# Layer 1 of a graph network: edge products are laid into the gather's destination and the gather adds to them

## Chip, core and metric

One core of one Trainium2 chip. The metric is device time in microseconds (us) of one execution, median of several runs. Engines are named as in the profile: PE (TensorE), DVE (VectorE), ACT (ScalarE), POOL (GpSimd, which also issues the gathers), SP (SyncE, which issues the plain transfers).

## What is computed

Four layers on a graph of 3125 nodes with 256 features and 50,000 edges sorted by target. The change is in layer 1, a graph transformer with 8 heads of 32:

```
h   = relu(layernorm(x))
q, k, v, skip = h@Wq.T+bq, h@Wk.T+bk, h@Wv.T+bv, h@Wskip.T+bskip
e   = edge_attr @ We.T                       # per edge, 64 -> 256
k_e = k[src] + e ;  v_e = v[src] + e
a   = sum_c(q[dst] * k_e) / sqrt(32)          # per head
w   = softmax of a over the edges of one dst
x  += segment_sum(v_e * w, dst) + skip
```

## The kernel before

`dense_phase(layer=1)` computes q, k, v and skip in 25 tiles of 125 nodes. Queries stay in SBUF. A table in HBM (`table_kv`) gets, for each node, the 256 keys and then, in 8 heads of 33 columns, value minus key and a column of ones (`moved`): 520 words a row.

`blend_phase` then walks the edges. The edge list is padded to 448 steps of 125 edges; G = 4 steps are a block, B = 4 blocks a chunk, so there are 28 chunks and 112 blocks. Per block:

- POOL gathers four times 128 rows of the table into `rows` (L1335), two chunks ahead at most: it waits until the block that used the buffer two chunks before is summed (`summed`).
- PE, `ask`: `queries` times a one-hot matrix gives q[dst] in PSUM (L1436); ACT copies it to `asked` (L1397).
- PE, `keys`: attributes times We (L1449) and, on top of it in the same PSUM bank `ps_k`, identity times the gathered keys (L1452): k[src] + e. In fp32 each product is two recorded MATMULs.
- DVE, `offer`: keys times queries (L1530), and (v - k) + (k + e) (L1532), which is the value with its edge part. `judge` sums the first per head (L1538).
- PE, `part`: a small product for layer 3 (L1462), moved out by DVE `lift`.
- Once per chunk a running maximum per target is carried over the steps: transposes on PE, scans on DVE (L1594 to L1626), ended by L1603, which signals `peaked`.
- DVE, `message`: values and ones times the weight (L1552); PE, `total`: one-hot times messages (L1471, signals `summed`); DVE, `add`: into the accumulator (L1564).

These are pipelined by hand. Each engine's `body(c, h)` runs the four slots b = 0 to 3 of chunk c in one loop; in slot b PE asks and keys the block LEAD = 6 blocks ahead and totals block b. SP loads, per chunk, the one-hot places (488 KB), lanes and flags, then for each block two pieces of attributes of 62.5 KB (L1224, semaphore `attrset[b]`). Its order for chunk c:

```
if not known(c, 2):
    keep(c - 2, h)
    sp.wait_ge(broad, (c - 1) * B)
    sp.wait_ge(peaked, c - 1)
...
sp.dma_start(places[:, h], targets[...]).then_inc(loaded[h], 16)
load_borders(sp, borders, lane, flag, c, h, laned)
...
    load_attributes(nc, sp, c, b, word, [...], attr_t, attrset[b])
```

`peaked` reaches c - 1 in DVE's slot b = 3 of the loop three chunks before c.

## Time and profile before

| | |
|---|---|
| median of 3 runs | 3252.54 us (3248.59 to 3256.95) |
| profiled execution, its own time | 3248.09 us |
| its span, first to last instruction | 3246.0 us |
| mean granted TensorE clock | 0.865 |
| busy over the span: PE, DVE, ACT, POOL | 78%, 71%, 52%, 47% |
| blend stage of layer 1 | about 760 to 1736 us |

The busy shares are means over stages with different limits, so the blend stage is read by itself. A row's "idle before" is the time in which the engine had nothing to do just ahead of that group, and the arrow names what ended the wait; "issue" is time with no visible cause.

### The profile page before, as it was taken

The numbers are of one execution on the slowest core, as the hardware profiler recorded it, in microseconds if no ns is written. First come the engines' busy times: TensorE is split into PE (matmuls) and PEld (weight loads), VectorE is DVE, ScalarE is ACT, GpSimd is POOL, SyncE is SP. The second block draws the span as 40 slices with busy tenths as digits, with TensorE's granted clock in tenths as the row PEclk, the third lists the DMA queues.
The fourth block names the chain that finished last, engine by engine and source line by source line (L and its number), as shares of the span: only waits on it lengthen the run. The fifth ranks groups of instructions, "written<-read, shape, count | busy, mean of one in ns | idle before, by whom it ended". The sixth has DMA issues, their size and how long they took to land. (4 is left out here: it accounts for less than half of the span.)

```text
span 3246.0 us, 56122 instructions
## 1 busy us (share of the span) xinstructions
PE 2527.9 (78%) x12612; PEld 1928.6 (59%) x12613; DVE 2300.0 (71%) x5860; ACT 1696.6 (52%) x4048; POOL 1516.6 (47%) x1759
## 2 busy tenths in 40 slices
PE   2999998596999999999984488887860577878870
PEld 1888887444666666666663366666650455666650
DVE  4788887574788788778775367676778466766767
ACT  1666665322555555555552466666641466666651
POOL 1333333103444555455440377777730377777740
PEclk9999999798999999999996678778875777878885
DMA  2100000225556666565640355555522455555521
GB/s 68 24 10 8 10 9 9 60 67 177 152 159 166 161 164 165 153 168 159 164 122 24 113 134 139 137 139 137 139 60 35 116 142 142 142 142 141 142 64 39
DMA packets 186874, 349.20 MB, mean 108 GB/s; under 512 B 74641, under 2 KB 117034, under 8 KB 186507
## 3 DMA queue, kind: packets, MB, share of 16 engines
q0 software_dynamic: 83520, 249.39, 30.4%
q1 hardware_dynamic: 103239, 98.62, 10.5%
q14 instruction: 84, 0.68, 0.1%
q8 instruction: 31, 0.51, 0.1%
HBM read 325.45 MB, written 22.44 MB: 107 GB/s over the span
## 5 line engine op out<-in xcount | busy, mean ns | idle before, releaser
L1759 POOL DMA_INDIRECT t_rows<-table_h,t_istage x896 | 854.6, 954 | 266.0 <-issue 248.6
L1846 PE MATMUL t_pso<-t_rows,t_hot 125*125 125x272 f32 (+1 forms) x1792 | 597.3, 489 | 104.6 <-DVE t_rows L1885 64.3
L1335 POOL DMA_INDIRECT b_rows<-table_kv,b_istage x448 | 458.8, 1024 | 378.5 <-PE b_pso L1471 252.9
L1846 PEld LDWEIGHTS t_pso<-t_rows,t_hot 125*125 125x125 f32 x1792 | 402.7, 236 | 202.5 <-issue 105.5
L1397 ACT COPY b_asked<-b_psq 125x512 f32<-125x512 f32 x224 | 131.1, 585 | 427.6 <-PE b_psq L1436 427.6
L1885 DVE TENSOR_TENSOR t_rows<-t_rows,t_psm 125x1056 f32<-125x1056 f32 x224 | 276.7, 1235 | 63.5 <-issue 63.4
L1832 PE MATMUL t_pss<-node_scores,t_hot_t 125*125 x1792 | 266.2, 279 | 33.7 <-ACT t_hot_t L1790 31.1
L1832 PEld LDWEIGHTS t_pss<-node_scores,t_hot_t 125*125 125x125 f32 x1792 | 260.5, 225 | 49.1 <-issue 44.1
L1797 ACT ACTIVATE t_hot<-con_iota,g_dstl 125x125 f32<-125x125 f32 x896 | 280.3, 384 | 0.0
L1895 DVE TENSOR_TENSOR acc<-acc,t_pso 125x272 f32 (+1 forms) x448 | 192.7, 430 | 118.2 <-DVE acc L1895 69.1
L1436 PE MATMUL b_psq<-queries,b_hot_t 125*125 x896 | 235.6, 386 | 45.4 <-issue 23.7
L1452 PE MATMUL b_psk<-b_rows,con_ident 125*125 125x256 f32 x896 | 256.4, 409 | 0.0
L1471 PE MATMUL b_pso<-b_rows,b_hot 125*125 125x264 f32 x896 | 236.0, 408 | 17.4 <-DVE b_rows L1552 17.4
L1530 DVE TENSOR_TENSOR b_rows<-b_psk,b_asked 125x1024 f32<-125x1024 f32 x112 | 136.5, 1218 | 151.2 <-PE b_psk L1452 151.2
L1788 ACT ACTIVATE t_hot_t<-t_places,t_minus 125x500 f32<-125x500 bf16 x224 | 156.5, 699 | 108.5 <-PE t_pss L1832 77.8
L1436 PEld LDWEIGHTS b_psq<-queries,b_hot_t 125*125 125x125 f32 x896 | 163.1, 190 | 76.1 <-issue 51.6
L1452 PEld LDWEIGHTS b_psk<-b_rows,con_ident 125*125 125x125 f32 x896 | 151.7, 189 | 89.2 <-issue 76.2
L1148 PE MATMUL d_pso<-wt,d_ht 128*125 128x512 f32 (+1 forms) x400 | 160.1, 545 | 44.6 <-DVE d_stage L1010 19.1
L1471 PEld LDWEIGHTS b_pso<-b_rows,b_hot 125*125 125x125 f32 x896 | 164.8, 194 | 46.3 <-issue 19.7
L1449 PE MATMUL b_psk<-we,b_attr 64*125 64x256 f32 x896 | 158.8, 430 | 22.2 <-issue 12.6
L1790 ACT ACTIVATE t_hot_t<-t_hot_t,con_ones 125x500 f32<-125x500 f32 x224 | 159.4, 712 | 7.3
L1801 ACT ACTIVATE t_hot<-t_hot,con_ones 125x500 f32<-125x500 f32 x224 | 159.4, 712 | 7.3
(394 smaller groups left out, 4961.5 us busy)
## 6 DMA issues: line engine op xcount, KB each, us to landing
t_places<-targets SPq DMA_DIRECT2D x56, 488.3 KB
t_rows<-table_h,t_istage POOLq DMA_INDIRECT x896, 3.7
b_attr<-in_attr_t SPq DMA_DIRECT2D x224, 62.5 KB
b_places<-targets SPq DMA_DIRECT2D x28, 488.3 KB
b_rows<-table_kv,b_istage POOLq DMA_INDIRECT x448, 5.4
table_h<-d_stage SPq DMA_DIRECT2D x50, 132.8 KB
t_flag<-flags SPq DMA_DIRECT2D x56, 62.5 KB
table_kv<-d_moved SPq DMA_DIRECT2D x25, 128.9 KB
```

The lines of the kernel that those rows point to most:

```text
L1148: mm = pe.matmul(ps_o[u % 3][0:P, lo:hi], ht[:, u, a, :], weight[:, a, lo:hi], start=(a == 0), stop=(a == 1))
L1335: pool.indirect_dma_start(out=rows[:, h, s, :], out_offset=None, in_=table, in_offset=bass.IndirectOffsetOnAxis(ap=istage[:, h, s:s + 1], ...
L1436: mm = pe.matmul(ps_q[0:P, w * D:(w + 1) * D], hot_t[:, b % 2, v * PAIR + w, :], q, start=True, stop=True)
L1452: mm = pe.matmul(to(u), ident[0:P, 0:P], rows[0:P, h, b * G + u, 0:D], start=False, stop=True)
L1471: mm = pe.matmul(ps_o[0:P, at:at + MW], hot[:, h, b * G + u, :], rows[0:P, h, b * G + u, D:WIDE], start=u % PAIR == 0, stop=u % PAIR == PA ...
L1759: pool.indirect_dma_start(out=rows[:, r, s, :], out_offset=None, in_=table, in_offset=bass.IndirectOffsetOnAxis(ap=istage[:, r, s:s + 1], ...
L1790: act.activation(x, x, ACT.Relu, scale=-1.0, bias=con["ones"][0:P, 0:1]).then_inc(hot_ts, 1)
L1797: act.activation(hot[:, r, b * G + u, :], con["iota"][0:P, 0:P], ACT.Abs, scale=-1.0, bias=g["dstl"][:, bass.ds(n * G + u, 1)]).then_inc(d ...
L1832: mm = pe.matmul(expanded[:, b * G + u], hot_t[:, b % 2, u, :], ntab[:, bass.ds(ts[u // PAIR], 1), 0:nw].rearrange("p a d -> p (a d)"), st ...
L1846: mm = pe.matmul(ps_o[b % 2][0:P, at:at + mw], hot[:, r, b * G + u, :], rows[0:P, r, b * G + u, 0:mw], start=u % PAIR == 0, stop=u % PAIR ...
L1885: dve.tensor_tensor(v, v, weight[:, b * G:(b + 1) * G].unsqueeze(3).to_broadcast([P, G, H, HW]), ALU.mult).then_inc(mset, 1)
L1895: dve.tensor_tensor(row, row, ps_o[b % 2][0:P, v * 512:v * 512 + mw], ALU.add).then_inc(added, 1)
```

## The change

1. The table's row is keys and values side by side, 512 words, without ones; `moved`, its subtraction and one of the two stores of each tile go.
2. PE forms only the edge product (`edges`), two blocks earlier than `keys` did: REACH = 8 blocks ahead of the slot, where `ask` stays at 6. The identity products go.
3. The product is copied from PSUM twice into the block's rows, once for the keys and once for the values, 7 blocks ahead (`spread`): ACT's `lay` copies two halves for blocks 1 and 2, one for blocks 0 and 3, whose other half DVE copies (`lend`). Each copy reads 512 words a partition and writes 1024.
4. The gather takes 125 rows of 512 words and adds them to what lies there (`compute_op=ALU.add`); it waits for `laid` and, in blocks 0 and 3, `lent`.
5. `offer` is one multiplication, SBUF by SBUF, and waits for the gather; the addition goes. ACT writes the exponential weights straight into the rows' last 8 columns; messages have 32 columns a head, and the denominator is its own 8 columns.

```diff
...
                         dve.wait_ge(evac, n + 1)
-                        parts = lambda k: stage[:, u, k * D:(k + 1) * D].rearrange("p (h c) -> p h c", h=H)
-                        dve.tensor_tensor(moved[:, u, :].rearrange("p (h c) -> p h c", h=H)[:, :, 0:C], parts(2), parts(1), ALU.subtract).then_inc(lined, 1)
...
                             if layer == 1:
-                                sp.wait_ge(lined, n + 1)
-                                sp.dma_start(tables[0][bass.ds(n * P, P), 0:D], stage[:, u, D:2 * D]).then_inc(stored[u], 16)
-                                sp.dma_start(tables[0][bass.ds(n * P, P), D:D + MW], moved[:, u, :]).then_inc(stored[u], 16)
+                                sp.wait_ge(evac, n + 1)
+                                sp.dma_start(tables[0][bass.ds(n * P, P), :], stage[:, u, D:3 * D]).then_inc(stored[u], 16)
...
     WIDE = D + MW
+    REACH = 2 * B
+    SHARED = (0, B - 1)
...
         istage = sb("istage", [ROWS, 2, RUN], I32)
-        rows = sb("rows", [ROWS, 2, RUN, WIDE])
+        rows = sb("rows", [P, 2, RUN, WIDE])
...
         asked = sb("asked", [P, 2, G, D])
...
+        def lent_by(c, b):
+            return 2 * c + (2 if b else 1)
+        def spread(to, bank, h, b, v):
+            s = b * G + v * PAIR
+            edge = bank[0:P, v * 512:(v + 1) * 512].rearrange("p (u d) -> p u d", u=PAIR)
+            return to(rows[:, h, s:s + PAIR, 0:2 * D].rearrange("p u (k d) -> p u k d", k=2), edge.unsqueeze(2).to_broadcast([P, PAIR, 2, D]))
...
                     for b in range(B):
-                        if not known(c, 2):
-                            pool_wait(pool, summed, (c - 2) * B + b + 1)
+                        if b in SHARED:
+                            pool.wait_ge(lent, lent_by(c, b))
+                        pool_wait(pool, laid, c * B + b + 1)
...
                             s = b * G + u
-                            pool.indirect_dma_start(out=rows[:, h, s, :], out_offset=None, in_=table,
-                                                    in_offset=bass.IndirectOffsetOnAxis(ap=istage[:, h, s:s + 1], axis=0)).then_inc(gathered[h * B + b], 16)
+                            pool.indirect_dma_start(out=rows[:, h, s, 0:2 * D], out_offset=None, in_=table,
+                                                    in_offset=bass.IndirectOffsetOnAxis(ap=istage[0:P, h, s:s + 1], axis=0), compute_op=ALU.add).then_inc(gathered[h * B + b], 16)
...
+                def lay(c, h, b):
+                    n = c * B + b
+                    act.wait_ge(edged, n + 1)
+                    if not known(c, 2):
+                        act.wait_ge(summed, n - 2 * B + 1)
+                    if b not in SHARED:
+                        spread(act.copy, ps_k[b % 2], h, b, 1)
+                    spread(act.copy, ps_k[b % 2], h, b, 0).then_inc(laid, 1)
...
                     if v == 0 and (b >= 2 or not known(c, 1)):
-                        act.wait_ge(used, n - 1)
+                        act.wait_ge(multiplied, n - 1)
...
                     for b in range(B):
-                        here, ahead, hence = (block_at(c, h, b + k) for k in (LEAD, LEAD + 1, 1))
+                        here, ahead, hence, empty = (block_at(c, h, b + k) for k in (LEAD, LEAD + 1, 1, REACH - 1))
+                        if b == 0 and not known(c, 0):
+                            act.wait_ge(gapped, c + 1)
+                            act.activation(rows[:, h, :, 2 * D:WIDE], gap[:], ACT.Exp, scale=SCALE).then_inc(weighed, 1)
+                        if empty:
+                            lay(*empty)
...
                             ask(*here, 0)
-                        if b == 0 and not known(c, 0):
-                            act.wait_ge(gapped, c + 1)
-                            act.activation(weight[:], gap[:], ACT.Exp, scale=SCALE).then_inc(weighed, 1)
...
                 turn(0, 0, 0)
+                for b in range(B - 1):
+                    lay(0, 0, b)
...
-                def keys(c, h, b, w):
+                def edges(c, h, b, w):
...
-                        pe.wait_ge(gathered[h * B + b], (c - h) * 8 * G + 16 * G)
                         if b >= 2 or not known(c, 1):
-                            pe.wait_ge(used, n - 1)
+                            pe.wait_ge(laid, n - 1)
+                            if b == 2:
+                                pe.wait_ge(lent, lent_by(c, 0))
+                            elif b == 1:
+                                pe.wait_ge(lent, lent_by(c - 1, B - 1))
...
                         half = slice(v * ED, (v + 1) * ED)
-                        pe.matmul(to(v * PAIR + w), attr[half, b, w * P:(w + 1) * P], we[half], start=True, stop=False)
-                    for v in range(GP):
-                        u = v * PAIR + w
-                        mm = pe.matmul(to(u), ident[0:P, 0:P], rows[0:P, h, b * G + u, 0:D], start=False, stop=True)
+                        mm = pe.matmul(to(v * PAIR + w), attr[half, b, w * P:(w + 1) * P], we[half], start=True, stop=True)
                     if w == PAIR - 1:
-                        mm.then_inc(keyed, 1)
+                        mm.then_inc(edged, 1)
...
                     for b in range(B):
-                        here = block_at(c, h, b + LEAD)
+                        here, empty = (block_at(c, h, b + k) for k in (LEAD, REACH))
...
                             ask(*here, 0, word)
-                            keys(*here, 0)
+                        if empty:
+                            edges(*empty, 0)
...
                             ask(*here, 1, word)
-                            keys(*here, 1)
+                        if empty:
+                            edges(*empty, 1)
...
                 word = load_stairs(pe, g, 0)
+                for b in range(B - 1):
+                    for w in range(PAIR):
+                        edges(0, 0, b, w)
                 for b in range(LEAD - B):
-                    ask(0, 0, b, 0, word)
-                    keys(0, 0, b, 0)
-                    ask(0, 0, b, 1, word)
-                    keys(0, 0, b, 1)
+                    for v in range(GP):
+                        ask(0, 0, b, v, word)
                     part(0, 0, b)
+                for w in range(PAIR):
+                    edges(0, 0, B - 1, w)
...
                     n = c * B + b
-                    dve.wait_ge(keyed, n + 1)
+                    dve.wait_ge(gathered[h * B + b], (c - h) * 8 * G + 16 * G)
                     dve.wait_ge(copied, (n + 1) * GP)
-                    mine = rows[0:P, h, b * G:(b + 1) * G]
-                    k = ps_k[b % 2][0:P, :]
-                    dve.tensor_tensor(mine[:, :, 0:D], k.rearrange("p (u d) -> p u d", u=G), asked[:, b % 2], ALU.mult).then_inc(multiplied, 1)
-                    v = mine[:, :, D:].rearrange("p u (h c) -> p u h c", h=H)[:, :, :, 0:C]
-                    dve.tensor_tensor(v, v, k.rearrange("p (u h c) -> p u h c", u=G, h=H), ALU.add).then_inc(used, 1)
+                    k = rows[:, h, b * G:(b + 1) * G, 0:D]
+                    dve.tensor_tensor(k, k, asked[:, b % 2], ALU.mult).then_inc(multiplied, 1)
+                def lend(c, h, b):
+                    dve.wait_ge(edged, c * B + b + 1)
+                    spread(dve.tensor_copy, ps_k[b % 2], h, b, 1).then_inc(lent, 1)
...
                 def message(c, h, b):
-                    n = c * B + b
-                    dve.wait_ge(used, n + 1)
-                    v = rows[0:P, h, b * G:(b + 1) * G, D:].rearrange("p u (h c) -> p u h c", h=H)
-                    dve.tensor_tensor(v, v, weight[:, b * G:(b + 1) * G].unsqueeze(3).to_broadcast([P, G, H, HW]), ALU.mult).then_inc(mset, 1)
+                    mine = rows[:, h, b * G:(b + 1) * G]
+                    v = mine[:, :, D:2 * D].rearrange("p u (h c) -> p u h c", h=H)
+                    dve.tensor_tensor(v, v, mine[:, :, 2 * D:WIDE].unsqueeze(3).to_broadcast([P, G, H, C]), ALU.mult).then_inc(mset, 1)
...
                         if b == 0:
-                            dve.wait_ge(rescaled, c + 1)
+                            dve.wait_ge(rescaled, 2 * c + 2)
...
                                 first = nc.s_assert_within(now & 31, 0, NT - 1, skip_runtime_bounds_check_because="a count of NT - 1 borders")
-                                old = acc[:, bass.ds(first, 1), 0:MW].rearrange("p a (h c) -> p (a h) c", h=H)
+                                old = acc[:, bass.ds(first, 1), 0:D].rearrange("p a (h c) -> p (a h) c", h=H)
+                                share = acc[:, bass.ds(first, 1), D:MW].rearrange("p a h -> p (a h)")
...
                                     dve.wait_ge(added, c * B * GP)
-                                dve.scalar_tensor_tensor(old, factor.unsqueeze(2).to_broadcast([P, H, HW]), 1.0, old, ALU.add, ALU.mult).then_inc(rescaled, 1)
+                                dve.scalar_tensor_tensor(old, factor.unsqueeze(2).to_broadcast([P, H, C]), 1.0, old, ALU.add, ALU.mult).then_inc(rescaled, 1)
+                                dve.scalar_tensor_tensor(share, factor, 1.0, share, ALU.add, ALU.mult).then_inc(rescaled, 1)
...
                             message(c, h, b)
+                        if empty and empty[2] in SHARED:
+                            lend(*empty)
...
                     dve.tensor_copy(split[v * ED:(v + 1) * ED, v], we3[v * ED:(v + 1) * ED]).then_inc(setup, 1)
+                lend(0, 0, 0)
...
             we1, asks = fsb("we1", [128, D]), fsb("queries", [P, NT, D])
-            t1 = dram("table_kv", N, D + MW)
+            t1 = dram("table_kv", N, 2 * D)
...
```

The accumulator's denominator moves with it: the two readers in `dense_phase` take columns D to MW. SP's code in `blend_phase` is as before.

## Rows read from the trace of the kernel before

**Rows 1.** Windows, the blend stage alone: us, busy us of each engine (instructions), PEclk, DMA share.
```profile
812.00:1692.00 880.00, 836.21 (x4075) 599.04 (x4074) 703.03 (x1183) 470.58 (x1009) 433.25 (x441) 0.99 0.59 160
```

**Rows 2.** Groups by line and shape, 740 to 1750 us.
```profile
L1335 POOL DMA_INDIRECT b_rows<-table_kv,b_istage x448 | 458.8, 1024 | 378.5 <-PE b_pso L1471 252.9 <-issue 124.5 <-POOL b_istage L1320 1.2
...
L1452 PE MATMUL b_psk<-b_rows,con_ident 125*125 125x256 f32 x896 | 256.4, 409 | 0.0
...
L1552 DVE TENSOR_TENSOR b_rows<-b_rows,b_weight 125x1056 f32<-125x1056 f32 x112 | 140.1, 1251 | 1.3 <-ACT b_weight L1407 1.3
...
L1530 DVE TENSOR_TENSOR b_rows<-b_psk,b_asked 125x1024 f32<-125x1024 f32 x112 | 136.5, 1218 | 151.2 <-PE b_psk L1452 151.2
...
L1532 DVE TENSOR_TENSOR b_rows<-b_rows,b_psk 125x1024 f32<-125x1024 f32 x112 | 135.6, 1211 | 0.0
...
L1397 ACT COPY b_asked<-b_psq 125x512 f32<-125x512 f32 x224 | 131.1, 585 | 427.6 <-PE b_psq L1436 427.6
```

**Rows 3.** Waits of the engines, 740 to 1750 us: total us, times, longest.
```profile
DVE b_rows L1530 <- PE b_psk L1452: 151.2, 85, 16.1
```

**Rows 4.** Line L1603, all its instructions.
```profile
L1603 DVE TENSOR_TENSOR_SCAN b_most<-b_flag,b_init,b_run x28: 477/478/479, 808.4 to 1705.1; 128x125 f32<-128x125 bf16 x28
```

**Rows 5.** Waits of SyncE's queue, 760 to 1750 us.
```profile
SPq L1352 <- DVE b_most L1603: 335.8, 26, 16.4
```

**Rows 6.** Timeline of one chunk: start us, us, engine, line.
```profile
1199.87 2.02 PE L1471 MATMUL b_pso<-b_rows,b_hot 125*125 125x264 f32 x8
...
1202.67 0.94 POOL L1335 DMA_INDIRECT b_rows<-table_kv,b_istage  x1 [2.39 <-PE b_pso L1471]
...
1203.21 0.40 DVE L1614 COPY b_on<-b_lane_ends 1x8 f32<-1x8 f32 x1
...
1205.50 0.16 DVE L1626 TENSOR_SCALAR b_fade<-b_fade 1x8 f32<-1x8 f32 x1
...
1206.88 1.25 DVE L1552 TENSOR_TENSOR b_rows<-b_rows,b_weight 125x1056 f32<-125x1056 f32 x1
...
1208.94 0.48 DVE L1603 TENSOR_TENSOR_SCAN b_most<-b_flag,b_init,b_run 128x125 f32<-128x125 bf16 x1
...
1209.63 0.29 SPq L1353 DMA_DIRECT2D b_places<-targets  x1
...
1212.72 3.40 SPq L1224 DMA_DIRECT2D b_attr<-in_attr_t  x4
...
1213.80 1.13 PE L1452 MATMUL b_psk<-b_rows,con_ident 125*125 125x256 f32 x4
...
1214.77 1.03 PE L1436 MATMUL b_psq<-queries,b_hot_t 125*125 x4
...
1214.96 1.25 DVE L1552 TENSOR_TENSOR b_rows<-b_rows,b_weight 125x1056 f32<-125x1056 f32 x1
...
1215.22 1.80 POOL L1335 DMA_INDIRECT b_rows<-table_kv,b_istage  x1 [0.30 <-issue]
```

**Rows 7.** DMA queues, 1215.3 to 1218.6 us: packets, MB, share.
```profile
q1 hardware_dynamic: 329, 0.24, 28.4%
```

**Rows 8.** DMA issues of the page: times, median us to landing.
```profile
t_rows<-table_h,t_istage POOLq DMA_INDIRECT x896, 3.7
...
b_rows<-table_kv,b_istage POOLq DMA_INDIRECT x448, 5.4
```

**Rows 9.** DMA queues, 812 to 1692 us.
```profile
q0 software_dynamic: 33280, 110.78, 46.7%
q1 hardware_dynamic: 27189, 29.45, 12.6%
```

**Rows 10.** Window of 3 us in layer 2.
```profile
2015.00:2018.00 3.00, 3.00 (x12) 2.20 (x10) 2.49 (x6) 2.39 (x6) 2.30 (x3) 0.61 0.54 167
```

**Rows 11.** TensorE timeline, layer 2.
```profile
2014.29 3.58 PE L1846 MATMUL t_pso<-t_rows,t_hot 125*125 125x272 f32 x8 [1.53 <-ACT t_hot L1801]
...
2018.72 2.08 PE L1846 MATMUL t_pso<-t_rows,t_hot 125*125 125x272 f32 x8
```

More of the change, by code:

```diff
@@ L917, in dense_phase @@
         stage = sb("stage", [P, U, RW if layer > 1 else width])
-        moved = sb("moved", [P, U, MW]) if layer == 1 else None
         inv = sb("inv", [P, NT, H]) if settle else None
@@ L928, in dense_phase @@
             sem(n) for n in ("empty", "cleared", "lined", "slanted", "settled", "brought", "put"))
-        stores = 2 if layer == 1 else len(tables)
+        stores = len(tables)
         work = graph(ph) if graph else None
@@ L1061, in _ @@
                     t = Tally(dve, settled)
[L1062 removed]
+                    t.then(dve.tensor_scalar(inv[:], acc[:, :, D:MW], 1e-16, None, ALU.add))
                     t.then(dve.reciprocal(inv[:], inv[:]))
@@ L1065, in _ @@
                     dve.wait_ge(con["x_brought"], 16)
-                if layer:
-                    lines = moved if layer == 1 else stage
-                    dve.memset(lines[:, :, 0:MW].rearrange("p u (h c) -> p u h c", h=H)[:, :, :, C:HW], 1.0)
+                if layer > 1:
+                    dve.memset(stage[:, :, 0:MW].rearrange("p u (h c) -> p u h c", h=H)[:, :, :, C:HW], 1.0)
                 measure(0)
@@ L1573, in body @@
                     for b in range(B):
-                        here, kept_back, last = (block_at(c, h, b + x) for x in (LEAD, LEAD - 1, -1))
+                        here, kept_back, last, empty = (block_at(c, h, b + x) for x in (LEAD, LEAD - 1, -1, REACH - 1))
                         if last:
```

9 lines of the change are left out of this document (4 added, 5 removed).

## The prediction, made before the changed kernel ran

> **What bounds the kernel now.** I read the page first for the stages, and then only the blend stage, because nothing else of weight changes. Its window view [rows 1] shows PE busy for 836 of 880 us at a granted clock of 0.99, with DVE at 703, ACT at 471 and POOL at 433. So PE looks like the limit, and the waits agree: DVE waits 151 us in 85 waits for the identity product L1452 [rows 3], and the POOL and ACT rows idle for PE lines too [rows 2]. The pace comes from L1603, which runs once a chunk: 28 times from 808.4 to 1705.1 us, so (1705.1 - 808.4) / 27 = 33.2 us a chunk [rows 4]. The 880 us are therefore 26.5 chunks, with 31.6 us of PE, 26.5 of DVE, 17.8 of ACT each.
>
> The view that matters most for this change is another: SP's queue spends 336 us, 26 waits, on L1603 [rows 5]. That wait is `peaked`, and it holds back a chunk's places and attributes. It costs nothing now, because `keys` reads a chunk's first attributes two slots after the signal. The timeline of one chunk [rows 6] shows what hangs on it: L1603 ends at 1209.42, places are issued at 1209.63, the first attributes at 1212.72, four in 3.40 us.
>
> **What the change removes.** Two identity products of a slot half are four recorded MATMULs: L1452 starts at 1213.80 and the next product at 1214.77, so 0.97 us a half, 1.94 a block, 7.8 a chunk [rows 6]. If only PE counted, a chunk would take 33.2 - 7.8 = 25.4 us. DVE loses L1532, 4 x 1.21 = 4.8 us a chunk, and a thirtieth of L1552 [rows 2]. In the dense stage a subtraction and one store of each tile go; PE is the busier engine there, so I take nothing for it, and at most the 25 short subtractions, some 10 us, if PE does not cover them.
>
> **What it adds to the engines.** ACT copies six half banks a chunk. It now takes 0.585 us for 512 words [rows 2]; each new copy reads 512 and writes 1024, so between 0.585 and 1.17 us, 3.5 to 7.0 a chunk. ACT goes from 17.8 to at most 24.8. DVE copies two, at L1530's 1.22 (1024 words, one operand in PSUM): 26.5 - 4.8 - 0.2 + 2.4 + 0.3 (the second rescale and its wait) = 24.2. POOL has 16 x (1.024 + 0.30) = 21.2 [rows 2, 6]. No engine exceeds PE's 25.4. By the busy sums this is a large gain. I do not forecast it, because of the order of waits.
>
> **What it moves.** `edges` for block (c, 0) stands in PE's slot 0 of the loop right after the slot that signals `peaked` for SP's chunk c; `keys` stood two slots later. PE is in order: behind `edges` wait `ask` 1, `part` and `total` of that slot. And the gather, which was issued two slots before use with its buffer free, now stands between `laid` or `lent` (slot -7) and `offer` (slot -6). These two make one closed ring per chunk, from one L1603 to the next:
>
> 1. L1603's end to the first attributes landed. SP issues for 1209.42 to about 1214.4 (half of the 3.40 us), then the landing, behind 488 KB of places. The hardware queue still moved 0.24 MB from 1215.3 to 1218.6 [rows 7], which is nearly four pieces of 62.5 KB. I take 1218.4: 9.0 us. Low end: issue 5.0 plus 3.0, less than the 3.7 of a small gather [rows 8], 8.0; high 9.2.
> 2. Waiting PE does `edges` (at most the identity's 0.97), `ask` (1.03), ACT the copy (0.585) [rows 2, 6]: 2.6 us.
> 3. DVE: `offer` 1.22, `judge` 1.21, adds and lift 1.22 (L1626's end at 1205.66 to L1552 at 1206.88), `message` 1.25, `lend` 1.22 [rows 2, 6]: 6.1 us. `total` on PE runs beside the first two.
> 4. POOL wakes: L1471 ends at 1201.89, the gather starts at 1202.67, 0.78. Three more issues, 3 x 1.32 = 3.97. Landing of the last 5.4 [rows 2, 6, 8]: 10.15 us.
> 5. DVE, slot 2: `offer` and `judge` 2.43, carry chain L1614 to L1626, 1203.21 to 1205.66, 2.45 [rows 6]: 4.9 us.
> 6. Slot 3: adds 1.22, `message` to L1603's end, 1206.88 to 1209.42 [rows 6]: 3.75 us.
>
> The sum is 36.5 us. It contains little of PE, so the 7.8 us saved do not shorten it. Against 33.2 that is +3.3 us for each of 27 intervals: +89 us. Start and tail: the first gathers now wait for the first attributes and copies, but the first products did so before; I take 0, at most +10.
>
> **The one price the trace doesn't show** is the adding gather. The landing of a plain one of 2080 bytes a row is 5.4 us, of 1088 bytes 3.7 [rows 8]. Below: 3.7 instead of 5.4, -1.7 us; it can't be less than a plain one, but the 5.4 may contain a queue. Above: it reads its destination too, and the landing doubles, +5.4 us. I take 5.4, the row of the same size. From an unknown start-up of the adds come no gain and no cost in POOL's issue; were its 1.024 us half as long again, step 4 would get 1.5 us.
>
> **Costs that I leave to the range.** After an idle of 1.53 us PE's next eight products in layer 2 took 3.58 us against 2.08, in a window with a granted clock of 0.61, between the levels 1.2 and 2.4 GHz [rows 10, 11]. Here PE would idle about five us in step 2's place once a chunk, so its 2.0 us of work after it may take up to 4: up to +2.0. Against it, successive DVE instructions overlap by under 0.1 us, and `edges` may be shorter than identity: down to -0.8.
>
> A gather issue of 1.80 us began at 1215.22, under L1552, which multiplies two SBUF operands at 1214.96; the mean is 1.024 and undisturbed ones take 0.94 [rows 2, 6]. `offer` becomes such an instruction too, and it follows `lend` directly, as the gathers of step 4 do: up to +0.86 in the ring, +23 us. The Trainium skill's page "SBUF — State Buffer", section "Who interferes with whom", says that a VectorE instruction with two SBUF inputs contends with a GpSimd instruction that reads SBUF, while one with a PSUM operand does not. By that rule, this edit makes the interference twice as frequent; the trace agrees for L1552.
>
> **The rivals.**
>
> *Faster: the ring does not bind.* If attributes, copies and gathers come in time, the pace is the busiest engine's, 25.4 us, with idle starts about 26: 28 x (33.2 - 26) = -202, 3046 us. For it: every busy sum above. Against it: steps 1 and 4 together are 19 us of pure transfer and issue in which no engine's speed helps. It decides when the ring falls under 33.2 us; at 31 us the time would be 3189. Chance 0.16 for all faster than 3243.
>
> *The same.* All low ends together: 36.5 - 1.0 (step 1) - 1.7 (landing) - 0.8 = 33.0 us, about 3243 to 3263. Chance 0.08.
>
> *The adding gather loads the DMA engines.* The software queue has 46.7% of the 16 engines over 880 us for 110.78 MB [rows 9], in gathers of 128 x 2080 bytes 416 of them, so 0.467 x 880 / 416 = 0.99 us each on all engines. Doubled, it would want 93.4% beside the other queue's 12.6%, over 100%. Four gathers at 1.98 / 0.874 = 2.27 us come out slower than POOL's 1.32, so step 4 gets 4 x 0.95 + 1.0 = 4.8 us: a ring of 41.3, +219, 3467 us. For it: an add needs a second read. Against it: the share counts contended packets, and a chunk that is longer leaves more room. Chance 0.10, and 0.08 for something halfway.
>
> *Fewer engines.* With 125 rows instead of 128 each gather might run on five engines: 3.2 us instead of 0.99, +2.2 us in step 4, +59, 3401 us. The Trainium skill's page "DMA: Bandwidth & Descriptors", section "Why a DMA increments its semaphore by 16 and not by 1", says that the number of engines is the largest up to 16 that divides the slowest dimension, which for 125 is 5. No row here shows it for a gather. Chance 0.12.
>
> **How the numbers follow.** The likeliest is the ring as summed, 0.46: 3248.09 + 89 = 3337 us for the profiled execution, and as that one lies 4.5 us under the median of the runs, 3342 us. Its own range is 3290 to 3400. The measurement tells 0.3%, 10 us, from no change. Slower: 0.46 + 0.12 + 0.18 = 0.76; same 0.08; faster 0.16. The range for 8 in 10 leaves out the engine-bound case (0.14) and the fully doubled gather (0.06): 3225 to 3445 us.
>
> **What the profile would show.** Right: L1603's successor 36 to 37 us apart; PE idle some 5 us once a chunk, ended by the attributes' landing, at the first edge product of a chunk; the multiplication of `offer` waiting for gathers; PE busy below 80% of the stage and its clock under 0.99; SP's wait for the peak still there. Wrong if the chunk is near 26 us, if no wait ends on attributes, or if POOL's issues are much longer than 1.02 us. What would make the sum wrong by size: a gather landing far from 5.4 us.

## The result, and the profile after

The changed kernel takes 3844.9 us (median of 4 runs, 3839.0 to 3856.27) against 3250.86: a ratio of 1.1838, interval 1.1821 to 1.1855. The profiled execution took 3856.27 us. Slower was forecast, but 3342 us, and 3445 at most.

First the pace: all instructions of the scan that ends a chunk, which was L1603 and is now L1633.

```profile
L1633 DVE TENSOR_TENSOR_SCAN b_most<-b_flag,b_init,b_run x28: 477/478/479, 840.0 to 2292.3; 128x125 f32<-128x125 bf16 x28
```

A chunk takes (2292.3 - 840.0) / 27 = 53.8 us where it took 33.2 [rows 4]. That is 27 x 20.6 = 556 us of the 608 between the two profiled executions. The first scan starts 31.6 us later, and some 20 us are left behind the last one. So the loss is a loss a chunk, as forecast; it is six times as large.

The stretch from 900 to 1600 us (columns as in [rows 1]) and its software DMA queue (as in [rows 9]):

```profile
900.00:1600.00 700.00, 462.32 (x1578) 304.34 (x1579) 323.47 (x570) 306.08 (x572) 434.90 (x221) 0.69 0.66 97
```

```profile
q0 software_dynamic: 85635, 53.19, 58.1%
```

PE is busy for 66% of the stretch and its granted clock is 0.69; it was 95% and 0.99 [rows 1]. Nothing is at its limit. The software queue takes more of the engines (58.1% against 46.7%) and moves less: 53 MB in 700 us against 111 MB in 880.

The groups of lines, to be held against [rows 2], and the waits against [rows 3, 5], both from 740 to 2400 us; and what the gather's own line says of its issue (min, median and max in ns) and landing:

```profile
L1343 POOL DMA_INDIRECT b_rows<-table_kv,b_istage x448 | 931.1, 2078 | 306.4 <-issue 262.0 <-DVE b_rows L1321 33.2 <-ACT b_rows L1321 11.3
...
L1321 ACT COPY b_rows<-b_psk 125x1024 f32<-125x1024 f32 x168 | 164.0, 1011 | 180.4 <-PE b_pso L1492 165.7 <-PE b_psk L1473 14.6
...
L1555 DVE TENSOR_TENSOR b_rows<-b_rows,b_asked 125x1024 f32<-125x1024 f32 x112 | 137.2, 1225 | 645.6 <-DMA b_rows<-table_kv,b_istage 466.9 <-ACT b_asked L1414 178.6
```

```profile
DVE b_rows L1555 <- DMA b_rows<-table_kv,b_istage: 466.9, 75, 18.9
...
POOL b_istage L1327 <- DVE b_rows L1321: 267.6, 27, 11.4
...
PE b_psk L1473 <- DMA b_attr<-in_attr_t: 213.8, 35, 20.2
...
SPq L1360 <- DVE b_most L1633: 503.1, 26, 23.8
```

```profile
L1343 POOL DMA_INDIRECT b_rows<-table_kv,b_istage x448: 1982/1992/3024, 769.2 to 2265.8; - x150
...
DMA to landing us min/median/max: 7.9/10.0/15.7
```

The four waits are the ring of the prediction, each link by name: SP on the scan, PE on the attributes, POOL on the lent copy, DVE on the gather. Two numbers are not the prediction's: an issue takes 2.08 us in the mean (1.99 in the median) instead of 1.02 in the mean, and a gather lands after 10.0 us in the median instead of 5.4 [rows 2, 8].

One turn of the ring in the timeline:

```profile
1504.26 1.22 PE L1473 MATMUL b_psk<-we,b_attr 64*125 64x256 f32 x4 [9.95 <-DMA b_attr<-in_attr_t]
...
1509.42 3.86 PE L1492 MATMUL b_pso<-b_rows,b_hot 125*125 125x264 f32 x8
...
1515.55 1.22 DVE L1321 COPY b_rows<-b_psk 125x1024 f32<-125x1024 f32 x1
...
1517.34 2.02 PE L1492 MATMUL b_pso<-b_rows,b_hot 125*125 125x264 f32 x8
...
1517.85 1.99 POOL L1343 DMA_INDIRECT b_rows<-table_kv,b_istage  x1 [6.62 <-issue]
...
1524.74 2.81 POOL L1343 DMA_INDIRECT b_rows<-table_kv,b_istage  x1 [0.31 <-issue]
...
1537.54 1.22 DVE L1555 TENSOR_TENSOR b_rows<-b_rows,b_asked 125x1024 f32<-125x1024 f32 x1 [11.22 <-DMA b_rows<-table_kv,b_istage]
...
1546.03 0.48 DVE L1633 TENSOR_TENSOR_SCAN b_most<-b_flag,b_init,b_run 128x125 f32<-128x125 bf16 x1
...
1548.06 3.35 SPq L1225 DMA_DIRECT2D b_flag<-flags  x1
...
1552.88 3.37 SPq L1219 DMA_DIRECT2D b_attr<-in_attr_t  x4
...
1559.44 1.22 PE L1473 MATMUL b_psk<-we,b_attr 64*125 64x256 f32 x4 [4.91 <-DMA b_attr<-in_attr_t]
```

Read from the scan's end on: 12.9 us to the first edge product (1546.51 to 1559.44), 12.5 us from such a product to the end of the lent copy (1504.26 to 1516.77), 1.1 until POOL starts, 6.9 from its first issue to its fourth, 12.8 from there to the multiplication that waits for them, 9.0 to the end of the next scan. The eight products L1492 take 3.86 us in this turn and 2.02 in the next block. The granted clock is 0.50 (1.2 GHz) from 1486.0 to 1513.3 us, through the 9.95 us in which PE waits and the 9.0 us of products after it, and 1.00 (2.4 GHz) for the next block. It had fallen before that wait began, after shorter waits of PE (2.44 and 1.10 us).

### The profile page after: what moved, and what is told of

Its sections match the earlier page's. It is cut to its first block and busy times, and to the rows that moved or that the text cites. A ratio compares the mean times of both kernels' runs of the same rounds, so it can differ in the third digit from the quotient of the medians.

```text
span 3854.5 us, 54513 instructions
## 1 busy us (share of the span) xinstructions
PE 2630.2 (68%) x11716; PEld 1946.0 (50%) x11717; DVE 2245.1 (58%) x5806; ACT 1858.9 (48%) x4216; POOL 1993.9 (52%) x1759
## 5 line engine op out<-in xcount | busy, mean ns | idle before, releaser
L1343 POOL DMA_INDIRECT b_rows<-table_kv,b_istage x448 | 931.1, 2078 | 306.4 <-issue 262.0
L1555 DVE TENSOR_TENSOR b_rows<-b_rows,b_asked 125x1024 f32<-125x1024 f32 x112 | 137.2, 1225 | 645.6 <-DMA b_rows<-table_kv,b_istage 466.9
L1457 PE MATMUL b_psq<-queries,b_hot_t 125*125 x896 | 323.4, 495 | 80.8 <-issue 44.7
L1492 PE MATMUL b_pso<-b_rows,b_hot 125*125 125x264 f32 x896 | 361.0, 571 | 24.9 <-DVE b_rows L1578 24.9
L1473 PE MATMUL b_psk<-we,b_attr 64*125 64x256 f32 x896 | 199.8, 533 | 213.8 <-DMA b_attr<-in_attr_t 213.8
L1916 DVE TENSOR_TENSOR t_rows<-t_rows,t_psm 125x1056 f32<-125x1056 f32 x224 | 276.8, 1236 | 33.2 <-issue 33.1
L1457 PEld LDWEIGHTS b_psq<-queries,b_hot_t 125*125 125x125 f32 x896 | 202.7, 245 | 166.8 <-issue 133.2
L1492 PEld LDWEIGHTS b_pso<-b_rows,b_hot 125*125 125x125 f32 x896 | 241.3, 283 | 85.6 <-issue 24.7
L1321 ACT COPY b_rows<-b_psk 125x1024 f32<-125x1024 f32 x168 | 164.0, 1011 | 180.4 <-PE b_pso L1492 165.7
L1473 PEld LDWEIGHTS b_psk<-we,b_attr 64*125 64x125 f32 x896 | 85.1, 231 | 314.1 <-issue 274.3
L1590 DVE TENSOR_TENSOR acc<-acc,b_pso 125x264 f32 x224 | 95.9, 428 | 153.3 <-PE b_pso L1492 76.9
```

Of the source, the lines that this page charges most:

```text
L1321: return to(rows[:, h, s:s + PAIR, 0:2 * D].rearrange("p u (k d) -> p u k d", k=2), edge.unsqueeze(2).to_broadcast([P, PAIR, 2, D]))
L1343: pool.indirect_dma_start(out=rows[:, h, s, 0:2 * D], out_offset=None, in_=table, in_offset=bass.IndirectOffsetOnAxis(ap=istage[0:P, h, s: ...
L1457: mm = pe.matmul(ps_q[0:P, w * D:(w + 1) * D], hot_t[:, b % 2, v * PAIR + w, :], q, start=True, stop=True)
L1473: mm = pe.matmul(to(v * PAIR + w), attr[half, b, w * P:(w + 1) * P], we[half], start=True, stop=True)
L1492: mm = pe.matmul(ps_o[0:P, at:at + MW], hot[:, h, b * G + u, :], rows[0:P, h, b * G + u, D:WIDE], start=u % PAIR == 0, stop=u % PAIR == PA ...
L1916: dve.tensor_tensor(v, v, weight[:, b * G:(b + 1) * G].unsqueeze(3).to_broadcast([P, G, H, HW]), ALU.mult).then_inc(mset, 1)
```

## The experiments

A chunk is always (last minus first start of the scan's line) / 27. Results with an interval are the median of several runs; four runs (before_add, add_128, add_128_attr, attr_first) were timed once.

### The ring with a plain gather: plain_gather, plain_128, plain_128_attr

plain_gather takes `compute_op` away, so the edge products are overwritten and left out.

```diff
-    in_offset=...(ap=istage[0:P, h, s:s + 1], axis=0), compute_op=ALU.add)
+    in_offset=...(ap=istage[0:P, h, s:s + 1], axis=0))
```

> The changed kernel with a gather that overwrites instead of adding; it leaves the edge products out of keys and values, all instructions and waits stay. If the price of the add is what the ring of waits passes on, POOL's issue falls from 1.99 to about 0.95 us, the landing from 10 to 4 to 6 us, and a chunk from 53.8 to the forecast's 36 to 37 us: about 3330 us (3290 to 3400), still over the kernel before. Rival: the ring is not a limit of its own and the engines set the pace once the add is gone: 26 to 28 us a chunk, 3050 to 3110 us. Rival: the 125 rows (in place of 128) are what is dear: issue and landing stay, over 3700 us.

3490.43 us, ratio 1.0738 (1.0718 to 1.0758), 41.1 us a chunk: over the forecast, because the 125 rows are dear too. plain_128 also gathers 128 rows again (rows 125 to 127 belong to no edge; rows 96 to 127 are cleared once at the start):

```diff
-    rows = sb("rows", [P, 2, RUN, WIDE])        # gather: ap=istage[0:P, h, s:s + 1]
+    rows = sb("rows", [ROWS, 2, RUN, WIDE])     # gather: ap=istage[:, h, s:s + 1]
```

> The changed kernel with a plain gather of 128 rows, so with the transfer as it was before; edge products are left out of keys and values. The forecast's ring, with the transfer that it assumed: 36 to 39 us a chunk, 3330 to 3400 us (the half clock after the wait for attributes adds 2 to 4 us that the sum left out). Rival: with the old transfer the ring does not bind: 26 to 28 us a chunk, about 3070 us.

3402.12 us, 1.0468 (1.0451 to 1.0486), 37.4 us a chunk. The forecast of the ring was 36.5. plain_128_attr also cuts the ring's first link: SP loads a chunk's first attributes ahead of its wait for the scan.

```diff
+    attributes(c, 0, word)
     keep(c - 2, h)
     sp.wait_ge(broad, (c - 1) * B)
     sp.wait_ge(peaked, c - 1)
...
-    for b in range(B):
+    for b in range(1, B):
```

> plain_128 with SP loading the first block's attributes of a chunk ahead of its wait for the peak. If the ring through the peak is what binds, it loses step 1 (9.0 us): what is left is the loop over three slots from total to copy, gather, offer and total, some 27 to 30 us a chunk: 3080 to 3180 us. Rival: the attributes' wait only covers another one of the same length: within 1% of plain_128.

3323.85 us, 1.0209 (1.0182 to 1.0236), 34.9 us a chunk, where 27 to 30 were expected. The link was worth 2.5 us. From the scan's end to the chunk's first edge product it is now 3.5 us instead of 7.8, and from `offer` to the scan's end 11.6 instead of 8.5, so most of the gain is lost there. Which loop sets the pace then is not shown.

### The adding gather: before_add, add_128, add_128_attr, attr_first

before_add puts the add alone into the kernel before: rows cleared once, so keys and values are sums over all that was gathered before them.

```diff
+    pool.memset(rows[:], 0.0)
...
-    in_offset=...(ap=istage[:, h, s:s + 1], axis=0))
+    in_offset=...(ap=istage[:, h, s:s + 1], axis=0), compute_op=ALU.add)
```

> The kernel before with a gather of 128 x 520 words that adds to what lies in the rows (cleared once at the start, some 15 us); keys and values are then wrong sums, the instructions are the same. If the add's price is a property of the adding gather, POOL's issue is 2.0 us here too: 16 x 2.3 = 36.8 us a chunk on POOL, which becomes the bound: at least 33.2 + 3.6 us a chunk, 3360 us, and up to 3500 if the transfers queue. Rival: the add is dear only with 125 rows: issue 0.95, and 3250 to 3270 us.

3603.95 us in one run, beside 3247.78, and 45.6 us a chunk: the add costs 12.4 us a chunk in the old order too, where no such ring exists. The forecast was 3360 to 3500. add_128 is the changed kernel with 128 rows, edge products and all:

> The changed kernel with an adding gather of 128 rows instead of 125; the result is the same. If the row count spreads the transfer over too few engines, the landing falls from 10 to some 6 to 7 us, and with the ring's 27 passes the time falls by 80 to 150 us to about 3700 to 3770. If the add alone is dear: within 1% of 3845 us.

3581.48 us in one run, 44.4 a chunk: the three rows are worth 263 us, not 80 to 150. Its gather line beside that of plain_128, and the queues of the two from 900 to 1600 us, first add_128:

```profile
L1344 POOL DMA_INDIRECT b_rows<-table_kv,b_istage x448: 1540/1550/2576, 773.6 to 2002.9; - x150
...
q0 software_dynamic: 36069, 65.68, 63.7%
```

and plain_128:

```profile
L1344 POOL DMA_INDIRECT b_rows<-table_kv,b_istage x448: 941/949/1979, 776.0 to 1808.4; - x150
DMA to landing us min/median/max: 3.5/3.7/4.4
...
q0 software_dynamic: 24048, 78.86, 39.7%
```

In 700 us there are 700 / 44.4 x 16 = 252 gathers of the one and 299 of the other. So an adding gather has 143 packets and takes 0.637 x 700 x 16 / 252 = 28.3 us of engine time; a plain one has 80 packets and 14.9 us. In the trace a plain gather's packet carries two rows (4096 bytes, 229 ns in the mean), an adding one's carries one row (2048 bytes, 218 ns): half the bytes, the same time, twice the number.

With the attributes first, add_128_attr and attr_first (the latter with the changed kernel's 125 rows):

> The changed kernel with 128 rows and the attributes first. The result is the same as the reference's. add_128 took 44.4 us a chunk; without the wait for attributes 36 to 40, at POOL's own 16 x 1.86 = 30 us at best: 3350 to 3450 us. Rival: the DMA engines are the limit of the adding gather (64% busy for it, 10% for the rest): the time stays over 3530.

> The changed kernel (adding gather, 125 rows) with the attributes first. If the ring through the peak is the only limit, a chunk falls from 53.8 to some 43 us: about 3560 us. Rival: the three-slot loop with 9 us of issue and 12 of landing takes over: (9.2 + 12 + some 12) / 3 x 4 = 44 us and more: 3600 to 3700.

3446.88 and 3738.1 us (one run each, beside 3252.63), 38.7 and 49.3 us a chunk. Cutting the first link gives 5.7 and 4.5 us a chunk with the add, against 2.5 without, and does not rescue the change. add_128_attr came out inside its forecast, attr_first 38 us above the upper one.

### The number of rows: before_125, plain_112, add_112

before_125 is the kernel before with its plain gather over 125 rows, and nothing else:

```diff
-    out=rows[:, h, s, :] ... ap=istage[:, h, s:s + 1]
+    out=rows[0:P, h, s, :] ... ap=istage[0:P, h, s:s + 1]
```

> The kernel before, its gather cut from 128 to 125 rows; the result is the same. If fewer rows mean fewer DMA engines, the landing rises from 5.4 us towards 8 and the time stays within 0.3%, since a gather has two slots of 8 us there. Rival: nothing changes in the landing; same time.

3430.45 us, 1.0568 (1.0536 to 1.0601), 39.8 us a chunk. Both forecasts said "the same"; leaving out three padding rows costs 180 us. To tell "not all rows" from "a number that does not divide by 16", the same two gathers of the changed kernel over 112 = 16 x 7 rows:

> The changed kernel with a plain gather that brings 112 rows of each block half instead of 125; it leaves out the edge products and the rows 112 to 124. If 125 rows are dear because they don't divide evenly over the 16 DMA engines (125 = 16 x 7 + 13), 112 = 16 x 7 rows cost as 128 do: GpSimd's issue 0.95 us or less, landing 3.7, a chunk about 37 us, 3390 to 3405 us. If any gather of fewer than all rows is dear, whatever the number, 112 go as 125: issue 1.2 us, a chunk 41 us, about 3490.

> The changed kernel with its adding gather over 112 rows; it leaves out the keys and values of rows 112 to 124. With 125 rows a chunk takes 53.8 us and with 128 rows 44.4, where the plain gather has 41.1 and 37.4: together the two edits cost 16.4, apart 3.7 and 7.0. If the number that doesn't divide over 16 engines is what makes both together so dear, 112 rows go as 128: issue 1.55 us, 44 us a chunk, about 3580 us. If it is any gather of fewer than all rows, 112 go as 125: issue 2.0 us, 54 us, about 3840.

| rows | plain: issue, chunk, time | adding: issue, chunk, time |
|---|---|---|
| 128 | 0.95 us, 37.4, 3402 | 1.55 us, 44.4, 3581 |
| 112 | 0.93 us, 37.4, 3381 | 1.49 us, 44.0, 3577 |
| 125 | 1.21 us, 41.1, 3490 | 1.99 us, 53.8, 3845 |

Ratios of the 112s: 1.0419 (1.0397 to 1.0440) and 1.1004 (1.0977 to 1.1032). They go as 128 does; 125 alone is dear. The queues show the odd number. before_125, and then plain_112, 900 to 1600 us:

```profile
DMA packets 81871, 94.30 MB, mean 135 GB/s; under 512 B 50018, under 2 KB 61231, under 8 KB 81863
...
q0 software_dynamic: 63289, 73.85, 38.4%
```

```profile
q0 software_dynamic: 24007, 68.86, 36.3%
```

A plain gather of 125 rows has 225 packets (63289 in 281 gathers), one of 112 or 128 has 80. In the trace nearly all the extra ones are of 8 bytes and 8 to 9 ns each; the adding gather of 125 rows has 411 packets (85635 in 208), 276 of them of 8 bytes. The engine time of a gather hardly moves (15.3 us against 14.9 plain, 31.3 against 28.3 adding), so the packets' own time is not the cost.

What does change is how many engines share one gather. Take the starts of the software queue after a pause of over 1.5 us, and count the packets of over 1000 bytes that are in flight at a time in the first microsecond. With plain gathers of 125 rows they are 6 at most (53 starts in before_125, 47 in plain_gather); with 128 and 112 plain rows the peak is 15 to 19 (53 starts each in plain_128 and plain_112). With the add the peak is mostly 6 and never over 8 for 125 rows (25 starts in after), and 15 to 23 for 128 and 112. The queue in one such microsecond of plain_gather (1364.4 to 1365.4), plain_128 (1313.2 to 1314.2) and plain_112 (1310.4 to 1311.4):

```profile
q0 software_dynamic: 121, 0.05, 32.4%
```

```profile
q0 software_dynamic: 60, 0.23, 91.0%
```

```profile
q0 software_dynamic: 70, 0.22, 74.2%
```

Records of neighbouring packets overlap a little: 16 engines show up to 19. So 6 in flight stand for about five engines, and five of 16 are 31%.

### Issue or transfer: before_pause, plain_128_pause, before_slow, plain_128_slow

The adding gather is dearer in two ways: POOL issues it in 1.55 instead of 0.95 us, and its packets load the engines. These four are meant to lengthen the issue alone. They, and the last of the next part, ran on chips on which the kernel before took 3613 to 3615 us instead of 3248 to 3253, so they are compared by ratios and with each other only.

```diff
     pool.indirect_dma_start(...)
+    for _ in range(12):
+        pool.nop(nofuse=True)
```

> The kernel before with 12 empty instructions behind each of its gathers on GpSimd: the gather stays plain, of 128 rows, and lands in 3.7 us; only the time from one issue to the next grows, by what the profile will show (some 0.3 to 1 us). With the adding gather in the same place a chunk grew from 33.2 to 45.6 us, where issues are 0.6 us longer and the block lands 2.5 us later. If GpSimd's longer issue alone does that, a pause of p us a gather costs 12 x p / 0.6 us a chunk here: 45 us at 0.6. If the loaded DMA engines and the later landing do it, a pause of 0.6 costs at most the four issues of one block, 2.4 us a chunk, and the time stays under 3320 us.

> The changed kernel with a plain gather of 128 rows (edge products left out) and the same 12 empty instructions behind each gather. Without them a chunk takes 37.4 us, with the adding gather of 128 rows 44.4. If step 4 of the ring (four issues in a row and the landing) prices the issue, a pause of p us adds 4 x p a chunk: 39.8 us at 0.6, about 3465 us; the rest of the 7 us of the adding gather is then the landing and the loaded DMA engines. If GpSimd's time as a whole bounds a chunk, it adds 16 x p less what GpSimd now waits, which is 10 us a chunk: nothing at 0.6.

0.9994 (0.9979 to 1.0009) and 1.0446 (1.0408 to 1.0484). The empty instructions told nothing of the question: in the timeline of before_pause 0.30 us lie between two issues, as they did.

```profile
1002.83 1.17 POOL L1335 DMA_INDIRECT b_rows<-table_kv,b_istage  x1 [0.30 <-issue]
```

So a memset of 128 x 512 stands there, into a tile that nobody reads; each waits for the one before it:

```diff
+    pool.memset(waste[:], 0.0).then_inc(wasted, 1)
```

> The kernel before with a memset of 128 x 512 values behind each of its gathers on GpSimd (by a memset of 1360 values that takes 1.23 us and one of 448 that takes 0.46, some 0.5 us). The 12 empty instructions tried first left 0.30 us between two issues, as before, and so lengthened nothing. The gather stays plain, of 128 rows, landing in 3.7 us. With the adding gather a chunk grew from 33.2 to 45.6 us, where issues are 0.6 us longer and the block lands 2.5 us later. If GpSimd's longer issue alone does that, a chunk takes 43 to 46 us here. If the transfers themselves do it (adding rows, later landing), the longer issue costs at most the four of one block, 2.4 us a chunk, and the ratio to before stays under 1.025.

> The changed kernel with a plain gather of 128 rows (edge products left out) and the same memset behind each gather. Without it a chunk takes 37.4 us, with the adding gather of 128 rows 44.4. If step 4 of the ring prices the issue (four in a row), it adds four times 0.5 to 0.6 us a chunk: some 39.7 us, a ratio of about 1.067 against 1.047. If it adds nearly all of the 7 us, GpSimd's time bounds a chunk, and the landing has no part in it.

```profile
1117.08 0.95 POOL L1335 DMA_INDIRECT b_rows<-table_kv,b_istage  x1 [0.17 <-POOL b_waste L1339]
1118.03 0.54 POOL L1339 MEMSET b_waste<- 128x512 f32 x1
1118.74 0.95 POOL L1335 DMA_INDIRECT b_rows<-table_kv,b_istage  x1 [0.17 <-POOL b_waste L1339]
```

Now issues are 1.66 us apart instead of 1.25 (the adding ones are 1.85 apart), 6.6 us more of POOL a chunk. before_slow has a ratio of 1.0051 (1.0031 to 1.0071) and 35.9 us a chunk, against 34.4 for before_pause. If the issue made before_add's 12.4 us, two thirds of them should be here; it is 1.5 at most. So in the old order the cost is not in the issue, and what is left of the add is its transfers. plain_128_slow stands at 1.0471 (1.0445 to 1.0497), where 1.067 was expected, beside 1.0446 for plain_128_pause, 40.7 us a chunk beside 40.5. That looks like nothing, but the two differ in PE's clock as well.

By the ring's steps (the medians of the table below) the memset makes the first four issues 1.6 us longer (5.9 against 4.3) and step 1 2.8 us (10.0 against 7.2), and the landing 0.8 shorter (3.5 against 4.3). Steps 5 and 6 go the other way: 8.7 us against 11.8. In plain_128_pause PE's products of the carry, on which the scan depends, stand at a granted clock of 0.50 in 18 of 20 chunks, behind a wait for ACT like this one; in plain_128_slow in 1 of 20, in plain_128 in none.

```profile
1227.60 2.06 PE L1463 MATMUL b_psq<-queries,b_hot_t 125*125 x4 [4.10 <-ACT b_asked L1419]
```

So what the longer issues cost in the ring this pair can't tell: a second stretch at half clock in the run beside it stands against them.

### TensorE's clock: plain_128_warm, plain_128_warm9

plain_128 with products that fill PE's wait for a chunk's first attributes; edge products are left out as there. The wait for attributes moves behind those for `laid` and `lent`.

```diff
-    pe.wait_ge(attrset[b], c * 16 * GP + 16 * GP)
...
+    if b == 0 and not known(c, 2):
+        for k in range(24):                     # 9 in plain_128_warm9
+            pe.matmul(ps_k[0][0:P, 0:P], ident[0:P, 0:P], ident[0:P, 0:P], start=True, stop=True)
+    pe.wait_ge(attrset[b], c * 16 * GP + 16 * GP)
```

> The changed kernel with a plain gather of 128 rows (edge products left out) and 24 products of the identity with itself ahead of TensorE's wait for a chunk's first attributes, written to the bank that the edge products then overwrite. If the half clock after that wait costs 3 to 4 us of the ring a chunk, a chunk falls from 37.4 us to about 34.5 and the time from 3402 to about 3320 us. If the clock doesn't matter there, or the products delay the edge products by as much as they win, the time stays within 3390 to 3440 us.

3375.3 us, 1.0384 (1.0356 to 1.0412), 37.1 us a chunk against 37.4. By the stages below it did what it should and cost what it gave: 8.3 us instead of 12.3 from the edge product to the end of the lent copy, and 11.5 instead of 7.8 until the edge product starts. The granted clock at the chunk's first edge product is 1.00 in all 20 chunks, where it is 0.50 in all 20 of plain_128.

> As the run with 24 identity products ahead of TensorE's wait for a chunk's first attributes, with 9 of them (the changed kernel with a plain gather of 128 rows, edge products left out). The 24 took 5.4 to 6.3 us where the wait was 4.0, and a chunk stayed at 37.1 us against 37.4. Nine take some 2.3 us and end inside the wait. If the half clock behind the wait costs some 2 us of the ring, as the one chunk read from the trace says (10.3 us from the attributes to the end of the lent copy at half clock, 8.3 at full), a chunk falls to about 35.4 us and the time to about 3350. If nine don't hold the clock, or it doesn't matter, the time stays within 0.5% of 3402 us.

1.0372 (1.0340 to 1.0403), and 3748.5 us against plain_128_pause's 3781.4 on the same chip, 39.3 us a chunk against 40.5. Filling the wait gives about 1.2 us a chunk, less than the 2 expected. Nine products hold the clock at 1.00 up to the edge product in 16 of 20 chunks.

### The old order without identity products: dve_adds

PE forms the edge product alone; DVE adds it to the gathered keys ahead of its multiplication, and so DVE instead of PE waits for the gather; the table holds plain values.

```diff
-    pe.wait_ge(gathered[h * B + b], (c - h) * 8 * G + 16 * G)
-    pe.matmul(..., start=True, stop=False)
-    mm = pe.matmul(to(u), ident[0:P, 0:P], rows[0:P, h, b * G + u, 0:D], start=False, stop=True)
+    mm = pe.matmul(..., start=True, stop=True)
...
+    dve.wait_ge(gathered[h * B + b], (c - h) * 8 * G + 16 * G)
+    dve.tensor_tensor(mine[:, :, 0:D], mine[:, :, 0:D], k.rearrange("p (u d) -> p u d", u=G), ALU.add)
-    dve.tensor_tensor(mine[:, :, 0:D], k.rearrange("p (u d) -> p u d", u=G), asked[:, b % 2], ALU.mult)
+    dve.tensor_tensor(mine[:, :, 0:D], mine[:, :, 0:D], asked[:, b % 2], ALU.mult)
```

> The kernel before, without its identity products: TensorE makes the edge products alone, and VectorE adds them to the gathered keys in an instruction of its own ahead of the product with the queries; the table holds values as they are. The gather stays plain, of 128 rows, in its old order. TensorE loses some 3 us a chunk and VectorE gets four times about 1.2 us and loses nothing. If TensorE's work bounds a chunk of 33.2 us, it falls to about 31.5 and the time to about 3200 us; if VectorE's does, or a chain through it, a chunk grows by 1 to 4.8 us, to 3280 to 3380 us.

3271.22 us, 1.0075 (1.0056 to 1.0093), 34.1 us a chunk, between the two forecasts. Even in the old order, dropping the identity products does not pay with DVE's addition in their place. No version that ran beats the kernel before by more than the noise.

## Why the prediction was wrong in size

The ring's stages, each read off the traces of 20 chunks (from the 5th to the 24th scan) and given as medians in us, so that they add up only nearly. The first row is the end of the scan to the first edge product, and so on around.

| step | forecast | plain_128 | plain_gather | add_112 | add_128 | after |
|---|---|---|---|---|---|---|
| 1, to the edge product | 9.0 | 7.8 | 8.5 | 10.8 | 11.4 | 13.4 |
| 2 and 3, to the end of `lend` | 8.7 | 12.3 | 12.5 | 12.5 | 12.3 | 12.5 |
| 4, POOL starts | 0.8 | 0.9 | 1.0 | 0.9 | 0.9 | 1.1 |
| 4, first to fourth issue | 4.0 | 4.2 | 5.1 | 6.2 | 6.1 | 6.9 |
| 4, from there to `offer` | 5.4 | 4.1 | 5.9 | 5.6 | 5.8 | 11.8 |
| 5 and 6, to the scan's end | 8.65 | 8.5 | 8.6 | 8.6 | 8.4 | 8.4 |
| whole | 36.5 | 37.7 | 41.0 | 44.5 | 44.5 | 54.1 |

**What was right.** The busy sums promised 25.4 us a chunk and did not decide. The ring decides: its waits stand in the profile after, plain_128 runs at 37.4 us against the 36.5 summed, and taking its first link away shortens it. That the two sums lie so near is luck in part: steps 2 and 3 are 3.6 us longer than forecast, step 1 and the landing together 2.5 shorter. The copies cost what was said (ACT 1.01 us, DVE 1.22), steps 5 and 6 are right to 0.3 us in every kernel of the table, and PE lost its full clock.

**The step that failed** is "The one price the trace doesn't show", inside step 4. It took the plain gather's 5.4 us for the landing and no cost in POOL's issue. Step 4 was 10.15 us and is 19.8: 2.9 more from the first to the fourth issue, 6.4 more in landing. That is 9.7 of the 17.6 us by which the ring is longer than its sum; 4.4 more are in step 1 and 3.8 in steps 2 and 3. The bound of a doubled landing was there (10.8, measured 11.8 from the last issue) but was weighed as unlikely, and no bound was given for the issue beyond 1.5 us.

**Two rivals were both true**, where the chances had treated them as exclusive. *The adding gather loads the DMA engines*: it forecast twice the engine time of a gather, and 28.3 us against 14.9 is 1.9 times. Its ring was put at 41.3 us, and add_128 has 44.4. From plain_128 to add_128 step 1 grows by 3.6 us, the four issues by 1.9, the landing by 1.7. Step 1, which the rival left as it was, grows between the issue of the attributes and the edge product (4.4 to 8.0 us), while SP issues as before. That the attributes wait for engines which the adding gathers load fits this, and is not shown by a run of its own. In the changed kernel SP is late too: from places to attributes 5.4 us instead of 3.1, of which the issue of the flags takes 3.35 in the turn above (0.4 in add_128). *Fewer engines* for 125 rows was put at +2.2 us; it is +3.7 with a plain gather and +9.4 with an adding one. By the Trainium skill's rule quoted there (page "DMA: Bandwidth & Descriptors", section "Why a DMA increments its semaphore by 16 and not by 1"), 112 and 128 rows should go alike and 125 not, and the runs agree on that much. The packets agree too: 125 rows never have more than 6 of the plain gather's large packets in flight where 112 and 128 have 15 to 19, which is about the five engines that the rival named. Its +2.2 us in the landing is +1.8 in plain_gather (5.9 against 4.1).

**The clock** was left to the range with at most +2.0 us. It is +4.0 in steps 2 and 3, by plain_128_warm's 8.3 us against 12.3. The sum had counted only the work right behind the wait; in the timeline, `edges` (1.22 us against 0.70), `ask`, `part` and `total` (3.86 against 2.02) all run at half clock, and DVE's adds wait for `total`, so it does not end "beside the first two". In the time of plain_128_warm this does not show, because the 24 products start the edge product 3.7 us later.

**The gather under `offer`**, put at up to +0.86 us, is small: in plain_128 an issue that starts under `offer` takes 1.37 us in the median (82 of 448) against 0.95 elsewhere, and the first to the fourth issue 4.2 against 4.0.

**In the sum of the whole** (medians of runs on several chips, the add over 128 rows timed once): 151 us come from the new order with its copies (3402.1 against 3250.9, forecast 89), 179 from the add over 128 rows (3581.5), 263 from 125 rows on top (3844.9).

**Why the two edits cost more together.** Alone they cost 3.7 and 7.0 us a chunk, both together 16.4. The table puts most of the excess in the landing (4.1, 5.9, 5.8, then 11.8), and add_112 shows that it belongs to the number 125. An estimate from the queues' figures gives the direction: the add nearly doubles a gather's engine time, and with 125 rows about five engines share it instead of 16, so the two multiply. A plain gather then takes 15.3 / 5 = 3.1 us instead of 14.9 / 16 = 0.9, an adding one 31.3 / 5 = 6.3 instead of 28.3 / 16 = 1.8. The differences are 2.1 and 4.5 us, and the landing grows by 1.8 and 6.0.

**Open.** The 1.5 us between that estimate and the adding gather's landing have no run of their own. How much of the ring's growth is POOL's longer issue is not settled either: the table shows 1.9 us of it from the first to the fourth issue in add_128, but what a longer issue does to step 1 was seen only beside a run with another clock.

## What to carry to other kernels

When a change moves a transfer from "issued long before use" to "issued between two dependent steps", sum the closed loop from a chunk to the next with every issue and landing in it; the busy shares say nothing about it. A transfer of a form that the trace does not contain (here: one that adds, and one over 125 rows instead of 128) is a price to measure alone before the kernel is built around it, and rivals that can both be true must be priced together as well. Keep padding rows in an indirect gather when they bring it to a multiple of 16: 112 and 128 rows were fast here and 125 was not, and no other number was tried.

## What the runs showed of the hardware

- An indirect gather of 125 rows of 2080 bytes instead of 128 takes POOL 1.21 us an issue instead of 0.95, has 225 packets instead of 80, and makes this kernel 5.7% slower. Gathers of 112 rows of 2048 bytes go as those of 128 (0.93 and 0.95 us an issue, 80 packets).
- A gather of 125 rows that starts on an idle queue has at most 6 large packets in flight, one of 112 or 128 rows 15 to 19 (plain): it is spread over about five engines instead of 16.
- An accumulating gather of 128 rows moves one row a packet instead of two in the same time a packet, takes POOL 1.55 us an issue (1.99 over 125 rows), and nearly doubles the queue's time a gather (28.3 us against 14.9). With 125 rows its landing is 11.8 us in the ring instead of 5.8.
- An issue of a gather that starts under DVE's product of two SBUF operands takes 1.37 us instead of 0.95 (plain_128) and 2.50 instead of 1.99 (after), in the median.
- Twelve empty instructions of POOL behind a gather's issue take no time that the trace shows: the next issue still follows after 0.30 us.
- In 20 chunks of plain_128 PE waits 2.4 to 6.5 us for the first attributes; the granted clock is 0.50 when it goes on, and comes back to 1.00 after 3.6 to 9.8 us, 8.5 in the median (after: waits of 4.1 to 9.9 us, then 3.5 to 10.1). With the wait filled by 24 products it is 1.00 at that point in all 20 chunks, and steps 2 and 3 take 8.3 us instead of 12.3.
